# Moving the second norm's scale and bias to ScalarE, the attention product and the key rounding to GpSimd, and keeping the last norm token by token, with new instruction orders

## The reference

```
def ffn(x):                                   # outer feed-forward, ternary weights
    h = gelu_exact(ternary(rmsnorm(x), w_up)) # 128 -> 512
    return ternary(rmsnorm(h), w_down)        # 512 -> 128
x = x + 0.5 * ffn(layernorm(x))
r = x
y = layernorm(x)
for i in range(8):                            # eight layers
    Q = elu(y @ Wq[i] + bq[i]) + 1;  K = elu(y @ Wk[i] + bk[i]) + 1;  value = y @ Wv[i] + bv[i]
    KV = sum over tokens of K * value;  Ksum = sum over tokens of K
    V = Q * KV / (Q * Ksum + 1e-6)
    y = ln(gelu(V @ Wo[i] + bo[i]) + y) * ln1_s[i] + ln1_b[i]      # first norm
    y = ln(gelu(gelu(y @ W1[i] + b1[i]) @ W2[i] + b2[i]) + y) * ln2_s[i] + ln2_b[i]   # second norm
x = r + y
x = x + 0.5 * ffn(layernorm(x))
```

## Time and profile before

| | |
|---|---|
| median of 3 runs | 893.63 us (893.29 to 893.81) |
| span of the profiled execution | 892.1 us |
| PE busy | 849.9 us, 95% |
| DVE busy | 833.4 us, 93% |
| ACT busy | 798.2 us, 89% |
| POOL busy | 444.1 us, 50% |

### The profile page before, as it was taken

One profiled execution on the slowest core, in us unless ns is written; L12 is line 12 of the kernel. 1 busy time (PEld: TensorE's weight loads), 2 busy tenths in 40 slices (PEclk: granted clock), 3 DMA queues, 4 the chain that ended last, 5 costly groups with the idle time before them and its releaser, 6 DMA issues. The chain is left out here.

```text
span 892.1 us, 14583 instructions
## 1 busy us (share of the span) xinstructions
PE 849.9 (95%) x3915; PEld 587.8 (66%) x3915; DVE 833.4 (93%) x3349; ACT 798.2 (89%) x1136; POOL 444.1 (50%) x561
## 2 busy tenths in 40 slices
...
DMA packets 19520, 12.06 MB, mean 14 GB/s; under 512 B 1160, under 2 KB 18288, under 8 KB 19440
## 3 DMA queue, kind: packets, MB, share of 16 engines
...
## 5 line engine op out<-in xcount | busy, mean ns | idle before, releaser
L2039 POOL TENSOR_TENSOR x_lo<-x_fm,x_hi 128x512 fp32r<-128x512 f32 x120 | 153.8, 1282 | 231.0 <-DVE x_hi L1526 231.0
L488 PE MATMUL bank<-h,w 128*128 128x512 f32 x512 | 255.6, 592 | 0.0
L1290 DVE TENSOR_SCALAR z<-bank,mv,rstd 128x128 f32<-128x128 f32 x512 | 173.8, 403 | 6.5 <-POOL rstd L2031 3.8
L973 ACT ACTIVATE h<-bank,par 128x512 f32<-128x512 f32 x256 | 170.0, 691 | 8.5 <-PE bank L395 7.2
L393 PE MATMUL bank<-x_hi,w_hi 128*128 128x512 f32 x256 | 159.0, 621 | 0.3
L2031 POOL TENSOR_TENSOR rstd<-ve,minus_half 128x4 f32<-128x4 f32 x128 | 133.9, 1046 | 12.0
L393 PE MATMUL bank<-x_hi,wqkv_hi 128*128 128x512 f32 x192 | 108.1, 563 | 5.1 <-DVE phi_k L1420 4.2
L1276 DVE BATCH_NORM_STATS2 st<-bank 128x6 f32<-128x128 f32 x512 | 110.1, 281 | 2.8 <-PE bank L387 2.7
L488 PEld LDWEIGHTS bank<-h,w 128*128 128x128 f32 x512 | 91.0, 189 | 31.2 <-issue 18.7
L394 PE MATMUL bank<-x_lo,w_hi 128*128 128x512 f32 x256 | 100.9, 394 | 0.0
L395 PE MATMUL bank<-x_hi,w_lo 128*128 128x512 f32 x256 | 100.9, 394 | 0.0
...
## 6 DMA issues: line engine op xcount, KB each, us to landing
...
```

The lines of the kernel that those rows point to most:

```text
L488: mm = pe.matmul(m.ps_o[:, :], m.w2[T.weights][:, c, :], m.h[:, T.par, c, :], start=c == 0, stop=c == FC - 1)
L973: act.activation(m.h[:, T.par, c, :], m.ps_h[c % 2][:, :], ACT.Gelu_apprx_tanh, bias=column(m, B1, T.layer, c, FC)).then_inc(s.gelu_h[T.pa ...
L1290: last = dve.tensor_scalar(dst[:, j, :], src(j), mv[:, j, 0:1], scale[:, j:j + 1], ALU.subtract, ALU.mult)
L2039: pool.tensor_tensor(m.x_lo[:, T.slot, :], m.x_fm[:, T.slot, :], m.x_hi[:, T.slot, :].bitcast(F32), ALU.subtract).then_inc(done, 1)
```

## The change

`full` of the second norm goes from DVE to ACT and uses the same instruction as the first norm's. `attend` goes from DVE to POOL, unchanged. `round_kq` (1024 columns on DVE) becomes `round_q` (512 columns, DVE) and `round_k` (512 columns, POOL), with two semaphores. `log_den` and `recip` have float constants for their biases; the columns `eps`, `zero`, `ln_eps` and the instruction that made `ln_eps` are gone. In the last layer the second norm stays with its tokens: `z` multiplies by a broadcast row of scales instead of `rstd`, `x_in` multiplies by `rstd` and adds to `x_tm` in four instructions, POOL has added the broadcast bias row to `x_tm` beforehand (`add_b`, eight instructions of 128x512), and `turn_z`, `full` and `enter` of the last layer are gone. All written-out orders are new. Cut to its core (the long lists of the opening and the closing are left out):

```diff
+LN_EPS = math.log(EPS_ATTN)
...
+    for row, v in ((m.last_s, d.ln2[0]), (m.last_b, d.ln2[1])):
+        sp.dma_start(row[:, :], v[LAYERS - 1:LAYERS, :].to_broadcast([P, P])).then_inc(s.last_scale, DMA)
...
     def turn_z(T, i):
+        if not T or i == 1 and T.layer == LAYERS - 1:
             return
...
-    def enter(F):
-        if not F:
-            return
-        emptied(pe, left, "k")
-        left["k"] = (F.f.x_in, F.n)
-        pe.wait_ge(s.x_full, JOBS - NT + F.n)
-        transpose_tile(pe, m.ps_k, lambda j: m.x_fm[:, F.t, j * P:(j + 1) * P], m).then_inc(F.f.turned_x, 1)
...
     else:
         turn_z(l(0, 1), 0)
+        turn_z(l(1, 3), 1)
+        up(l(1, 2), 2)
         up(l(1, 2), 3)
-        turn_z(l(1, 3), 1)
+        turn_y(l(0, 2), 1)
+        turn_y(l(1, 1), 0)
         project(l(1, 0), VALUE)
-        turn_y(l(0, 2), 1)
-        project(l(0, -1), KEY)
-        turn_y(l(1, 1), 0)
         project(l(0, -1), QUERY)
         down(l(1, 2), 0)
+        project(l(0, -1), KEY)
+        down(l(1, 2), 1)
         up(l(0, 1), 0)
-        down(l(1, 2), 1)
         down(l(1, 2), 2)
         project(l(0, -1), VALUE)
+        up(l(0, 1), 1)
         down(l(1, 2), 3)
-        project(l(1, -1), KEY)
-        project(l(1, -1), QUERY)
-        up(l(0, 1), 1)
-        up(l(0, 1), 2)
         turn_z(l(1, 1), 0)
         turn_z(l(0, 2), 1)
+        project(l(1, -1), KEY)
         project_o(l(0, 0))
+        up(l(0, 1), 2)
         up(l(0, 1), 3)
         turn_y(l(1, 2), 1)
+        project(l(1, -1), QUERY)
+        turn_y(l(0, 0), 0)
+        up(l(1, 1), 0)
         down(l(0, 1), 0)
-        turn_y(l(0, 0), 0)
         down(l(0, 1), 1)
         project_o(l(1, 0))
-        up(l(1, 1), 0)
         down(l(0, 1), 2)
         up(l(1, 1), 1)
         down(l(0, 1), 3)
-        up(l(1, 1), 2)
...
-            last = act.activation(m.rec[:, T.par, cols], m.phi_q[:, T.par, cols], ACT.Ln, bias=m.eps[:, 0:1],
+            last = act.activation(m.rec[:, T.par, cols], m.phi_q[:, T.par, cols], ACT.Ln, bias=EPS_ATTN,
                                   scale=m.ksum[:, T.par, b:b + 1])
...
-        act.activation(m.rec[:, T.par, :], m.rec[:, T.par, :], ACT.Exp, bias=m.ln_eps[:, 0:1], scale=-1.0).then_inc(s.recip, 1)
+        act.activation(m.rec[:, T.par, :], m.rec[:, T.par, :], ACT.Exp, bias=LN_EPS, scale=-1.0).then_inc(s.recip, 1)
...
     def full(T, i):
-        if not T:
+        if not T or i == 1 and T.layer == LAYERS - 1:
             return
...
     else:
+        gelu_o(l(1, 1))
+        gelu_h(l(1, 2), 1)
+        gelu_ff(l(0, 2))
+        full(l(0, 1), 0)
+        full(l(1, 3), 1)
+        gelu_h(l(1, 2), 2)
+        gelu_h(l(1, 2), 3)
+        log_den(l(0, 0))
         negative(l(0, -1), QUERY)
+        log_den(l(1, 0))
+        negative(l(0, -1), KEY)
         recip(l(0, 0))
         exp(l(0, -1))
-        log_den(l(1, 0))
         recip(l(1, 0))
         gelu_h(l(0, 1), 0)
         gelu_ff(l(1, 2))
+        gelu_h(l(0, 1), 1)
+        full(l(1, 1), 0)
+        full(l(0, 2), 1)
+        gelu_o(l(0, 0))
+        gelu_h(l(0, 1), 2)
+        gelu_h(l(0, 1), 3)
         negative(l(1, -1), KEY)
-        gelu_h(l(0, 1), 1)
-        gelu_h(l(0, 1), 2)
-        full(l(1, 1), 0)
-        gelu_o(l(0, 0))
         negative(l(1, -1), QUERY)
-        gelu_h(l(0, 1), 3)
         exp(l(1, -1))
-        gelu_o(l(1, 0))
         gelu_h(l(1, 1), 0)
-        gelu_h(l(1, 1), 1)
-        gelu_ff(l(0, 1))
-        gelu_h(l(1, 1), 2)
-        full(l(0, 0), 0)
-        gelu_h(l(1, 1), 3)
-        log_den(l(0, -1))
-        negative(l(0, -2), KEY)
...
-    def round_kq(T):
+    def round_q(T):
         if not T:
             return
         dve.wait_ge(s.exp_kq, T.n)
-        dve.tensor_scalar(m.e[:, T.par, :, :], m.e[:, T.par, :, :], 1.0, 1.0, ALU.subtract, ALU.add).then_inc(s.rounded, 1)
+        dve.tensor_scalar(m.e[:, T.par, QUERY, :], m.e[:, T.par, QUERY, :], 1.0, 1.0, ALU.subtract,
+                          ALU.add).then_inc(s.rounded_q, 1)
...
             return
+        if i == 1 and T.layer == LAYERS - 1:
+            if T.slot < 2:
+                dve.wait_ge(s.turned_z2, T.n - 2)
+            else:
+                dve.wait_ge(f[1].x_in, T.slot - 1)
+            dve.wait_ge(s.last_scale, DMA * 2)
+            dve.wait_ge(s.mv2, T.n)
+            dve.wait_ge(s.turned_y2, T.n)
+            for j in range(BLK):
+                last = dve.scalar_tensor_tensor(m.z[1][:, T.par, j, :], source(1)(j), m.mv[1][:, T.par, j, 0:1],
+                                                m.last_s[:, :], ALU.subtract, ALU.mult)
+            last.then_inc(s.z2, 1)
+            return
         reused(dve, T, (s.turned_z1, s.turned_z2)[i])
...
     def x_in(F):
+        dve.wait_ge(s.last_bias, F.n)
+        for j in range(BLK):
+            last = dve.scalar_tensor_tensor(m.x_tm[:, F.t, j, :], m.z[1][:, T.par, j, :], m.rstd[1][:, T.par, j:j + 1],
+                                            m.x_tm[:, F.t, j, :], ALU.mult, ALU.add)
+        last.then_inc(F.f.x_in, 1)
         if not F:
...
     else:
-        z(l(0, 3), 1)
         mean_v(l(1, 1))
-        sum_kv(l(0, 0))
-        attend(l(1, 1))
+        sum_value(l(0, 0))
+        neg_ksum(l(0, 0))
         residual(l(1, 3), 1)
+        over_ksum(l(0, 0))
         hi(l(1, 2), 0)
-        full(l(0, 3), 1)
+        hi(l(0, 3), 1)
         residual(l(0, 1), 0)
         stats(l(1, 3), 1)
-        hi(l(0, 3), 1)
         means(l(1, 3), 1)
-        sum_value(l(0, 0))
-        over_ksum(l(0, 0))
         stats(l(0, 1), 0)
+        mean_v(l(0, 0))
         means(l(0, 1), 0)
         z(l(1, 3), 1)
-        mean_v(l(0, 0))
+        round_q(l(1, 0))
         z(l(0, 1), 0)
-        round_kq(l(1, 0))
         residual(l(1, 1), 0)
+        phi_q(l(1, 0))
+        residual(l(0, 2), 1)
+        hi(l(0, 1), 0)
         phi_k(l(1, 0))
-        residual(l(0, 2), 1)
-        neg_ksum(l(1, 0))
-        full(l(1, 3), 1)
-        hi(l(0, 1), 0)
-        phi_q(l(1, 0))
-        sum_kv(l(1, 0))
-        over_ksum(l(1, 0))
-        hi(l(1, 3), 1)
         stats(l(0, 2), 1)
         stats(l(1, 1), 0)
+        means(l(1, 1), 0)
+        means(l(0, 2), 1)
+        sum_kv(l(1, 0))
+        hi(l(1, 3), 1)
+        z(l(1, 1), 0)
+        neg_ksum(l(1, 0))
         sum_value(l(1, 0))
-        attend(l(0, 0))
-        means(l(1, 1), 0)
-        round_kq(l(0, -1))
-        means(l(0, 2), 1)
+        z(l(0, 2), 1)
+        round_q(l(0, -1))
         phi_k(l(0, -1))
+        sum_kv(l(0, -1))
         phi_q(l(0, -1))
-        z(l(1, 1), 0)
-        neg_ksum(l(0, -1))
+        over_ksum(l(1, 0))
...
     def rstd(T, i):
-        reused(pool, T, (s.z1, s.z2)[i])
+        if i == 1 and T.layer == LAYERS - 1 and T.slot > 1:
+            pool.wait_ge(f[1].x_in, T.slot - 1)
+        else:
+            reused(pool, T, (s.z1, s.z2)[i])
         pool.wait_ge((s.ve1, s.ve2)[i], T.n)
...
+    def attend(T):
+        if not T:
+            return
+        reused(pool, T, s.proj_o)
+        pool.wait_ge(s.recip, T.n)
+        pool.wait_ge(s.neg_a, T.n)
+        for b in range(2):
+            cols = slice(b * SEQ, (b + 1) * SEQ)
+            last = pool.tensor_scalar(m.vf[:, T.par, cols], m.rec[:, T.par, cols], 1.0, m.neg_a[:, T.par, b:b + 1],
+                                     ALU.subtract, ALU.mult)
+        last.then_inc(s.v_ready, 1)
+    def round_k(T):
+        if not T:
+            return
+        pool.wait_ge(s.exp_kq, T.n)
+        pool.tensor_scalar(m.e[:, T.par, KEY, :], m.e[:, T.par, KEY, :], 1.0, 1.0, ALU.subtract,
+                           ALU.add).then_inc(s.rounded_k, 1)
+    def add_b(F):
+        pool.wait_ge(s.last_scale, DMA * 2)
+        pool.wait_ge(f[0].z_c, F.n)
+        pool.tensor_tensor(m.x_tm[:, F.t, :, :], m.x_tm[:, F.t, :, :],
+                           m.last_b[:, :].unsqueeze(1).to_broadcast([P, BLK, P]), ALU.add).then_inc(s.last_bias, 1)
...
     else:
+        low(l(1, 2), 0)
+        attend(l(1, 1))
+        split_next_w1(l(1, 2))
+        var_eps(l(1, 3), 1)
+        rstd(l(1, 3), 1)
         var_eps(l(0, 1), 0)
+        split_next_qkv(l(1, 2))
+        split_next_w1(l(0, 1))
         rstd(l(0, 1), 0)
+        split_next_qkv(l(0, 1))
+        round_k(l(1, 0))
         low(l(0, 3), 1)
-        split_next_qkv(l(0, 0))
-        split_next_w1(l(0, 0))
-        split_next_qkv(l(1, 0))
-        split_next_w1(l(1, 0))
         low(l(0, 1), 0)
-        low(l(1, 3), 1)
         var_eps(l(1, 1), 0)
         rstd(l(1, 1), 0)
         var_eps(l(0, 2), 1)
         rstd(l(0, 2), 1)
-        low(l(1, 1), 0)
-        var_eps(l(1, 2), 1)
-        rstd(l(1, 2), 1)
+        attend(l(0, 0))
+        round_k(l(0, -1))
+        low(l(1, 3), 1)
```

More of the change, by code:

```diff
@@ L1114, in scalar_tick @@
         log_den(Tile(2))
+        full(Tile(0), 0)
         recip(Tile(2))
-        full(Tile(0), 0)
         log_den(Tile(3))
+        recip(Tile(3))
+        gelu_o(Tile(2))
         negative(Tile(5), KEY)
-        recip(Tile(3))
-        log_den(Tile(4))
```

(29 more changed lines are left out.)

802 lines of the change are left out of this document (384 added, 418 removed).

## The result

The changed kernel took 994.21 us (median of 4 runs, 991.35 to 995.58) against 893.72 us: a ratio of 1.1115 (95% interval 1.1095 to 1.1135). It is 11% slower. The forecast was 882.5 us and the range ended at 897.

What follows compares the result with a forecast made beforehand. It took PE, DVE and ACT as nearly full in the periodic part, with ACT bounding after the change (22.3 us a tick). Periodic +3, opening -5, drain -9 made -11: 892.1 to 881, plus 1.5, 882.5 us; range 868 to 897.

Steps and rivals of the forecast that it cites:

- The price of GpSimd's instructions: POOL per tick: 0.45 us for each half of `attend`, 0.65 for each `round_k`, adding 3.1 us.
- Rival 1: Periodic part: POOL's order becomes a wait of PE, +0.9 us a tick, 905.6 us; chance 0.12.
- The sign that I had given for it: Periodic part: PE showing waits for `x_lo` in the middle would prove the prediction wrong; no size given.
- Which DVE's new slack of 22.3 - 19.1 = 3.2 us covers: DVE per tick: six wide instructions each wait half a `round_k` for the shared port, 2.0 us, hidden by slack.
- ACT's sum: ACT per tick without waits: 21.48 us, plus 1.32 for two `full`, less 0.58 for constant biases, makes 22.2 us.
- the 0.10 us for a bias: ACT per tick: each of six logarithms and exponentials gets 0.10 us shorter without its bias column, -0.58 us.
- the allowance of 0.3 for PE: PE per tick: same products, idle 0.7 of 632 us, so it cannot get much shorter; 0.3 us allowed.
- Rival 2: Periodic part: a constant bias brings nothing, ACT's sum is 22.8 us a tick, 896.6 us; chance 0.08.
- rival 3: Whole kernel: the three engines fit at 22.1 us a tick and the ends overlap better, 869.6 us; chance 0.18.
- rival 4: Periodic part grows by a few ACT waits (22.45 us, +7), the opening gives nothing, 894.6 us; chance 0.12.
- The drain: Drain with the last feed-forward: -9 us, 7.0 from PE's dropped transposes and 2 from its idle time.
- The opening: Opening: DVE loses 3.8 us of work and the first projections fill idle time, -5 us.

Runs made afterwards that it cites:

- run 5: The changed kernel with `attend` and the key rounding back on DVE, and `neg_ksum` and `sum_value` moved one call later, behind `z`: 895.94 us, ratio 1.0015.
- experiment 4: The changed kernel with `low(l(1, 3), 1)` moved ahead of `attend` and `round_k` in POOL's list: 1036.38 us.
- run 13: Kernel before with even tiles' second-norm `full` on ACT, constant biases, token-by-token last norm, changed drain order (`attend`, rounding on DVE), `add_b` in eight ticks: 890.82 us.
- run 1: The changed kernel with `attend` and the key rounding back on DVE, its new orders kept: 919.99 us, ratio 1.0291.
- run 8: The kernel before with only the second norm's `full` on ACT and constant biases: 904.61 us, ratio 1.0119.
- runs 12 to 14: Kernel before with even tiles' second-norm `full` on ACT, constant biases, token-by-token last norm, changed drain order, `add_b` in three placements: 890.26, 890.82, 887.82 us.
- run 7: The kernel before with only the token-by-token last norm, old orders, `add_b` at the end of POOL's list in eight ticks: 903.58 us, ratio 1.0105.
- experiments 1 to 3: The changed kernel with GpSimd edits back on DVE: both `attend` and key rounding, `attend` alone, key rounding alone: 919.99, 913.16, 912.28 us.

## Why the prediction was wrong

1. **The price of GpSimd's instructions: the step that failed.** "From above I take the two-input one, 1.28, and half of it, 0.64, for a half of `attend`", and "one input has less to read than two". They measured 1.93 and 1.19, above even the upper ends of 1.28 and 0.64: an instruction with two inputs is no upper bound on one with one input and two operations, of which there was no wide row. The added work was 4 x 1.19 + 2 x 1.93 = 8.6 us in a tick, not 3.1. The Trainium skill, GPSIMD Engine Reference, Elementwise — side-by-side cycle accounting, is right that such work is a loss against VectorE (0.42 us there for `round_q`); the estimate of 0.77 us from its best case was too low by a factor of 2.5, as the trace has 1.93.
2. **Rival 1 was what happened, at more than three times its price.** It was to decide from 1 us for a `round_k` on. I had 0.9 us in a tick for it and gave it 0.12; it took 3.1 (25.67 against 22.61 in run 5). I had looked at PE's wait for `low` only. The sign that I had given for it came true, PE waits 33.1 us of 400 for `x_lo`, but the loop also runs over `phi_k` and `rstd` (the waits after the change, and experiment 4), and POOL's idle time, 294 us of 632 before, was no cover: nearly all of it was waiting for DVE (150.7 and 60.9 us of 500).
3. **"Which DVE's new slack of 22.3 - 19.1 = 3.2 us covers": wrong.** I priced the lock on the wide instructions, at 2.0 us a tick, and covered it. Under the wide subtraction the small quotients paid up to 1.1 us each (experiment 5: 25 us), and slack elsewhere in DVE's list covered nothing (run 13: 6.6 us longer for 6.9 of stretch). But in the changed kernel the lock is small: `attend` and `round_k` hardly hold DVE up, in the periodic part the quotients meet almost no subtraction, and `hi` pays 9.7 us in all, 0.3 a tick. So this step was wrong and is not what made the loss. The loss on the quotients is what the new orders would have cost with attend and rounding left on DVE (run 1: 26 us over the kernel before).
4. **ACT's sum was right** (22.2 forecast, 22.3 measured), so were the 0.10 us for a bias (0.096 and 0.099), and no period came out under 22.15, inside the allowance of 0.3 for PE. Rival 2 falls with the one, rival 3 (22.1) with the other. But two full lists don't run at the larger sum: the period was 0.2 (run 8) and 0.3 us (run 5) above ACT's sum, where I took 0.1. Even without GpSimd's part the periodic part would have been 12.7 us longer (run 5), not 3, of which the old orders show 8.7 (run 8), and the time 895.9 us: near rival 4, not the forecast.
5. **The drain was right in size, not in cause: luck.** -9 forecast, -8.5 measured, -9.6 in runs 12 to 14. I had made 7.0 of it out of PE's transposes; the edit without its order gave 0.5 (run 7). What bounds the old drain the runs don't show; it shortens with the changed order.
6. **The opening was wrong:** -5 forecast, +8.0 measured. -2.4 is what it gave without the GpSimd edits (run 5), so these cost 10 us there; which of the two, or whether with `add_b`, isn't separated. From 100 to 131 us PE was busy for 20.2 us at a granted clock of 0.72, against 23.3 at 0.89 before.

The sum by these steps is +8.0 + 97.9 - 8.5 = 97.4 us. Run 5 has everything of the change but the two GpSimd edits, and one quotient's place, and the span of its profiled execution is that of the kernel before (892.1 us; its median time is 1.7 us above): ACT's load and the new orders took 12.7 us in the periodic part, and the two ends gave 2.4 and 10.3. So the 97.4 us go with GpSimd's edits, to within what the quotient's place does beside them, which wasn't run. They can't be shared out between the two (experiments 1 to 3).
